# Convolution as diagonal matmuls on TensorE, FP4 tiles cut into three pieces, and rows of B and C loaded per scan unit, in the state-space stage of a hybrid four-part kernel

## The reference, cut to what matters

```python
# L0_attn
xz = einsum('bld,ed->ble', x, W_in);  x_in, z = xz[..., :512], xz[..., 512:]
xc = conv_general_dilated(x_in^T, conv_w, (1,), [(3, 0)], feature_group_count=512) + conv_b   # 4 taps
u  = silu(xc)
x_dbl = einsum('bld,ed->ble', u, W_xproj)           # 16 columns of step size, 16 of B, 16 of C
delta = softplus(einsum('blr,dr->bld', delta_raw, W_dt) + b_dt)
def step(h, inp):                                   # scan over 512 tokens, state 512 x 16
    h = exp(d_t * A) * h + (d_t * u_t) * B_t
    y_t = sum_n h[:, n] * C_t[n]
y = (ys + D_param * u) * silu(z)
out = einsum('bld,ed->ble', y, W_out)
# L0_ffn
scale = max(max(abs(block of 16)) / 6, 1e-12);  q = nearest FP4 value of block / scale, times scale
h = silu(q(x) @ q(w_gate)) * (q(x) @ q(w_up));  out = q(h) @ q(w_down)     # 704 hidden columns
```

## Time and profile before

| | us |
|---|---|
| median of 3 runs | 3855.11 (3853.64 to 3855.38) |
| the profiled execution | 3852.84 |
| its span | 3850.7 |
| busy: PE, DVE, ACT, POOL | 3230.5, 2634.9, 1656.0, 1587.6 |
| first scan of the stage starts at | 124.44 |
| last gate_y of the stage starts at | 1574.76 |

### The profile page before, as it was taken

One profiled execution on the slowest core, in us unless ns is written; L12 is line 12 of the kernel. 1 busy time (PEld: TensorE's weight loads), 2 busy tenths in 40 slices (PEclk: granted clock), 3 DMA queues, 4 the chain that ended last, 5 costly groups with the idle time before them and its releaser, 6 DMA issues. The chain is left out here.

```text
span 3850.7 us, 48624 instructions
## 1 busy us (share of the span) xinstructions
PE 3230.5 (84%) x15980; PEld 1864.1 (48%) x15980; DVE 2634.9 (68%) x3666; ACT 1656.0 (43%) x4077; POOL 1587.6 (41%) x974
## 2 busy tenths in 40 slices
PE   2677787778787778599999959999999689999998
PEld 1224242424242434366666626666666355655665
DVE  6798989888888989477677725555555255555553
ACT  1554545454545454166555613333333133333332
POOL 1555554655455545200000035554455165555552
PEclk9889898988888888899999969999999899999999
DMA  1211111020202020100010020000000200000000
GB/s 47 99 44 61 47 58 72 32 93 11 93 11 93 11 88 11 41 29 26 22 33 27 12 75 12 21 16 16 16 16 11 68 17 22 22 22 22 22 16 17
DMA packets 82137, 141.89 MB, mean 37 GB/s; under 512 B 7730, under 2 KB 71302, under 8 KB 73878
## 3 DMA queue, kind: packets, MB, share of 16 engines
q1 hardware_dynamic: 73622, 132.66, 9.7%
q10 hardware_dynamic: 8448, 8.39, 0.7%
HBM read 119.54 MB, written 21.50 MB: 37 GB/s over the span
## 5 line engine op out<-in xcount | busy, mean ns | idle before, releaser
L902 PE MATMUL ps_y<-hb,ident 128*128 128x512 f32 x1024 | 588.0, 707 | 228.0 <-DVE hb L602 227.8
L492 POOL TENSOR_TENSOR hb<-bcB,du 128x1024 f32<-128x1024 f32 x256 | 604.3, 2374 | 374.0 <-PE ps_y L902 370.6
L592 DVE TENSOR_TENSOR_SCAN ps_dA<-ps_dA,hb 128x1024 f32<-128x1024 f32 x256 | 585.9, 2289 | 90.5 <-POOL hb L492 56.5
L902 PEld LDWEIGHTS ps_y<-hb,ident 128*128 128x128 f32 x1024 | 211.0, 221 | 510.3 <-DVE hb L602 305.3
L1691 POOL TENSOR_TENSOR c_pr<-c_pr,c_inv 128x512 f32<-128x512 f32 (+1 forms) x256 | 232.6, 934 | 411.6 <-DVE c_inv L1803 409.6
L2158 PE MATMUL c_ps_s<-c_hT,c_w 128*128 128x512 f32 x704 | 321.0, 603 | 17.2 <-DVE c_hid L1869 15.4
L1261 ACT ACTIVATE b_pr<-b_ps_s,b_negmax 128x256 f32<-128x256 f32 (+1 forms) x512 | 263.8, 527 | 164.8 <-DVE b_negmax L1175 162.9
L725 ACT ACTIVATE ps_dA<-delta,a_neg 128x511 f32<-128x511 f32 x512 | 329.4, 675 | 0.6
L1920 ACT ACTIVATE c_pr<-c_ps_s,c_negmax 128x256 f32<-128x256 f32 (+1 forms) x512 | 222.2, 446 | 246.5 <-DVE c_negmax L1798 246.5
L602 DVE TENSOR_TENSOR hb<-ps_dA,bcC 128x1024 f32<-128x1024 f32 x256 | 312.3, 1220 | 5.2
L1668 POOL TENSOR_TENSOR c_q_cos<-c_q_cos,c_q_sin 128x1024 f32<-128x1024 f32 x64 | 150.9, 2357 | 311.9 <-DVE c_q_sin L1777 311.9
(11 more groups left out here) (235 smaller groups left out, 6265.2 us busy)
## 6 DMA issues: line engine op xcount, KB each, us to landing
bcB<-bc_scratch SPq DMA_DIRECT2D x32, 1024.0 KB, 4.6
bcC<-bc_scratch SPq DMA_DIRECT2D x32, 1024.0 KB, 6.5
c_x<-stream_scratch SPq DMA_DIRECT2D x16, 512.0 KB, 5.0
c_xr<-stream_scratch SPq DMA_DIRECT2D x16, 512.0 KB, 4.4
xn<-in_x_dram SPq DMA_DIRECT2D x8, 512.0 KB, 7.2
xr<-in_x_dram SPq DMA_DIRECT2D x8, 512.0 KB, 4.0
x_scratch<-xr SPq DMA_DIRECT2D x8, 512.0 KB, 2.9
b_x<-x_scratch SPq DMA_DIRECT2D x8, 512.0 KB, 4.1
```

The costliest lines, as they stand in the source:

```text
L492: pool.tensor_tensor(hb[:, s % RING, :, :], bcB[:, states(g), :], bc(du[:, c % 2, :].unsqueeze(1), [P, NG, T]), ALU.mult)\
L592: dve.tensor_tensor_scan(flat(h_all), flat(h_all), flat(tile), 0.0, ALU.mult, ALU.add)\
L902: last = pe.matmul(ps_y[:, :], W["ident"][:, :], hb[:, r % RING, i, :], start=False, stop=(g == GROUPS - 1 and i == NG - 1))
```

## The change

It rewrites the schedule of the state-space stage and leaves the other stages as they are.

- **Convolution.** The four taps per chunk are no longer DVE operations. Sixteen diagonal matrices diag_c are built once, and per chunk PE runs four matmuls of 128 x 512 into ps_p; ACT applies silu straight from PSUM. Chunks 2 and 3 go through a side buffer u23 and are copied into u later (MOVE_U).
- **FP4 tiles.** fp4_steps becomes fp4_part: the maximum, scale and reciprocal in one unit, the division, exponent and step in the next, and the rounding in the third. This holds for the four h tiles and for x. h has two buffers.
- **B and C.** The buffers bcB and bcC hold four units of two rows each instead of all 16. Each unit loads its own two rows of B and two of C, 512 KB each, so 64 DMAs per batch instead of 8. B of unit s + 6 is issued in SP's step s after POOL has multiplied unit s + 2, C of unit s + 4 after DVE has weighed unit s.
- **Ring.** hb has 8 slots instead of 5.
- **Tables.** All pieces are moved. gate_y comes in the first unit of the next chunk instead of the second. Tiles 1 to 3 of the FP4 layer go to units 21 to 31; the last h tile is transposed in unit 4 of the next batch, and x1 moves to units 1, 2, 4 and 6. softplus of chunk 0 of the next batch is finished in this batch. silu(z) is taken straight from PSUM.

```diff
+def fp4_part(dve, st, rows, blk, work, p, n, part):
+    g = n // 16
+    amax, scale, inv = blk[0:p, 0, 0:g], blk[0:p, 1, 0:g], blk[0:p, 2, 0:g]
+    w = work[0:p, 0:n]
+    blocks = rows.rearrange("p (g e) -> p g e", e=16)
+    if part == 0:
+        st.link(dve.tensor_reduce(amax, blocks, AX.X, ALU.max, apply_absolute_value=True))
+        st.link(dve.tensor_scalar(scale, amax, 1.0 / 6.0, 1e-12, ALU.mult, ALU.max))
+        st.link(dve.reciprocal(inv, scale))
+        return st.done(dve.tensor_scalar(inv, inv, 1.0 - 2.0 ** -24, None, ALU.mult))
+    if part == 1:
+        dve.wait_ge(st.s, st.at(st.k))
+        st.link(dve.tensor_tensor(blocks, blocks, bc(inv.unsqueeze(2), [p, g, 16]), ALU.mult))
+        st.link(dve.tensor_scalar(w.bitcast(U32), rows.bitcast(U32), EXPONENT, None, ALU.bitwise_and))
+        return st.done(dve.tensor_scalar(w, w, 1.0, 1.5 * 2.0 ** 22, ALU.max, ALU.mult))
+    dve.wait_ge(st.s, st.at(st.k))
+    st.link(dve.tensor_tensor(rows, rows, w, ALU.add))
+    return dve.tensor_tensor(rows, rows, w, ALU.subtract)
...
-    RING = 5
-    GATE, SILU = [0, 3, 7, 11], [1, 3, 7, 11]
-    UP = [2, 4, 8, 12]
-    HIDDEN = [4 * t + 3 for t in range(TT)]
-    TURN_H, TAKE_H = [5, 9, 13, 17], [6, 10, 14, 18]
-    X1, TAKE_X1 = [3, 4, 7, 8], [5, 9]
-    Z, TAKE_Z = [20, 20, 24, 1], [21, 21, 26, 2]
-    STATS, TURN_XN, TAKE_XN = 6, 11, 12
-    XQ, TURN_XQ, TAKE_XQ = 16, 20, 21
-    XIN, TAKE_XIN = [16, 16, 18, 18], [17, 17, 19, 19]
-    CONV = [18, 19, 20, 21]
-    U, U3 = 22, 29
-    XD, TAKE_XD = 23, 24
-    DT = [25, 25, 27, 15]
-    ABS, LN, ADD = [26, 26, 28, 16], [27, 27, 3, 16], 20
-    SOFT = [("abs", 0), ("relu", 0), ("abs", 1), ("relu", 1), ("exp", 0), ("exp", 1), ("ln", 0), ("ln", 1),
-            ("abs", 2), ("relu", 2), ("exp", 2), ("ln", 2), ("abs", 3), ("relu", 3), ("exp", 3), ("ln", 3)]
+    RING, ROWS = 8, 4
+    GATE, SILU, UP = [0, 18, 22, 26], [1, 19, 23, 27], [2, 20, 24, 28]
+    HIDDEN = [3, 21, 25, 29]
+    TURN_H, TAKE_H = [9, 24, 28, 4], [10, 25, 29, 5]
+    X1, TAKE_X1 = [1, 2, 4, 6], [4, 8]
+    Z, TAKE_Z = [12, 22, 26, 0], [13, 23, 27, 1]
+    STATS, TURN_XN, TAKE_XN = 1, 6, 7
+    XQ, TURN_XQ, TAKE_XQ = 13, 30, 31
+    XIN, TAKE_XIN = [8, 8, 12, 13], [9, 9, 13, 14]
+    CONV, U = [10, 11, 14, 15], [11, 12, 15, 16]
+    MOVE_U = [20, 28]
+    XD, TAKE_XD = 17, 18
+    STORE = 9
+    DT, ABS, LN = [20, 21, 30, 8], [21, 22, 31, 9], [23, 23, 10, 10]
+    ADD = [26, 4, 13, 14]
+    SOFT = [("abs", 0), ("relu", 0), ("exp", 0), ("abs", 1), ("relu", 1), ("exp", 1), ("ln", 0), ("ln", 1),
+            ("abs", 2), ("relu", 2), ("exp", 2), ("abs", 3), ("relu", 3), ("exp", 3), ("ln", 2), ("ln", 3)]
...
-        bcB = sb("bcB", [P, NS, T])
-        bcC = sb("bcC", [P, NS, T])
+        bcB = sb("bcB", [P, ROWS, NG, T])
+        bcC = sb("bcC", [P, ROWS, NG, T])
...
+            def spread_b(n, s):
+                g = s % GROUPS
+                sp.dma_start(bcB[:, s % ROWS, :, :], bc_dram[n, 1 + g * NG:1 + (g + 1) * NG, :].unsqueeze(0).broadcast_to([P, NG, T]))\
...
+                for s in range(-2, SCANS):
+                    r = s + 2 + ROWS
+                    if r < SCANS:
+                        sp.wait_ge(dBu_ready.s, dBu_ready.at(b, s + 3))
+                        spread_b(b, r)
+                    elif r < SCANS + ROWS and more:
+                        sp.wait_ge(dBu_ready.s, dBu_ready.at(b, s + 3))
+                        if r == SCANS:
+                            sp.wait_ge(bc_out.s, bc_out.at(b + 1, 16))
+                        spread_b(b + 1, r - SCANS)
+                    r = s + ROWS
+                    if 0 <= s and r < SCANS:
+                        sp.wait_ge(weighed.s, weighed.at(b, s + 1))
+                        spread_c(b, r)
+                    elif 0 <= s and more:
+                        sp.wait_ge(weighed.s, weighed.at(b, s + 1))
+                        spread_c(b + 1, r - SCANS)
+                    if s == STORE and prev:
+                        tail(b - 1)
+                    if s == STORE + 2:
+                        sp.wait_ge(stored.s, stored.at(b, 0))
+                        sp.dma_start(xr[:, :, :], io["x"][b].rearrange("(t p) d -> p t d", p=P)).then_inc(xr_in.s, 16)
+                    if s == TAKE_XD + 1 and more:
+                        put_bc(b + 1)
...
-                        if c == 0:
-                            pool.wait_ge(bc_in[g // 2].s, bc_in[g // 2].at(b, 32))
+                        pool.wait_ge(b_in[s % ROWS].s, b_in[s % ROWS].at(b, landed(s)))
                         if s >= RING:
                             pool.wait_ge(summed.s, summed.at(b, s - RING + 1))
-                        else:
-                            pool.wait_ge(summed.s, summed.at(b, 0))
-                        pool.tensor_tensor(hb[:, s % RING, :, :], bcB[:, states(g), :],
+                        elif prev:
+                            pool.wait_ge(summed.s, summed.at(b - 1, SCANS + s - RING + 1))
...
-                if s in CONV:
-                    c = CONV.index(s)
-                    dve.wait_ge(xin_ready.s, xin_ready.at(n, c + 1))
-                    if c == IC - 1:
-                        to = u3[:, :]
-                        dve.wait_ge(u3_ready.s, u3_ready.at(n, 0))
-                    else:
-                        to = u[:, c, :]
-                        if not isinstance(n, int) or n:
-                            dve.wait_ge(du_ready.s, du_ready.at(n - 1, c + 1))
-                            dve.wait_ge(y0_done.s, y0_done.at(n - 1, c + 1))
-                    xs.link(dve.tensor_scalar(to, xin[:, c, 0:T], conv_w[:, c, 0:1], None, ALU.mult))
-                    for j in range(1, 4):
-                        ins = dve.scalar_tensor_tensor(to, xin[:, c, j:j + T], conv_w[:, c, j:j + 1], to,
-                                                       ALU.mult, ALU.add)
-                        if j < 3:
-                            xs.link(ins)
-                        else:
-                            ins.then_inc(cv_ready.s, 1)
+                    if s == XQ:
+                        dve.wait_ge(xn_ready.s, xn_ready.at(n, TT))
+                        dve.wait_ge(xn_turned.s, xn_turned.at(n, DC))
+                    last = fp4_part(dve, xs, rows, blk_x, work, P, TT * D, s - XQ)
+                    if s == XQ + 2:
+                        last.then_inc(xg_ready.s, 1)
...
+                    if HIDDEN[t] <= s < HIDDEN[t] + 3:
+                        rows, blk = h[:, t % 2, :], blk_h[:, t % 2, :, :]
+                        if s == HIDDEN[t]:
+                            if t == 0:
+                                hs.turn(b)
+                            dve.wait_ge(sg_ready.s, sg_ready.at(b, t + 1))
+                            dve.wait_ge(gated.s, gated.at(b, 2 * t + 2))
+                            if t:
+                                dve.wait_ge(h_turned.s, h_turned.at(b, 2 * t - 2))
+                            elif prev:
+                                dve.wait_ge(h_turned.s, h_turned.at(b - 1, 2 * TT - 2))
+                            dve.tensor_tensor(rows.rearrange("p (a n) -> p a n", a=2), ps_p[:, :, 0:HALF],
+                                              sg[:, :].rearrange("p (a n) -> p a n", a=2), ALU.mult).then_inc(h_ready.s, 1)
+                            dve.wait_ge(h_ready.s, h_ready.at(b, t + 1))
...
-                    if g == 1 and c:
+                    if g == 0 and c:
                         gate_y(b, c - 1)
-                    if s == 1 and prev:
+                    if s == 0 and prev:
                         gate_y(b - 1, IC - 1)
-                    ffn(b, s)
+                    ffn(b, s, prev)
...
+                    dve.wait_ge(c_in[s % ROWS].s, c_in[s % ROWS].at(b, landed(s)))
+                    dve.tensor_tensor(tile, h_all, bcC[:, s % ROWS, :, :], ALU.mult).then_inc(weighed.s, 1)
...
+                    if s == U[c]:
+                        act.wait_ge(cv_ready.s, cv_ready.at(n, c + 1))
+                        if c >= 2:
+                            to = u23[:, c - 2, :]
+                            act.wait_ge(u_moved.s, u_moved.at(n, 0))
+                        else:
+                            to = u[:, c, :]
+                            if not isinstance(n, int) or n:
+                                act.wait_ge(du_ready.s, du_ready.at(n - 1, c + 1))
+                                act.wait_ge(y0_done.s, y0_done.at(n - 1, c + 1))
+                        act.activation(to, ps_p[:, c % 2, :], ACT.Silu, bias=cols[:, 0, c:c + 1]).then_inc(u_ready.s, 1)
...
+                    if s == CONV[c]:
+                        pe.wait_ge(xin_ready.s, xin_ready.at(n, c + 1))
+                        for j in range(4):
+                            last = pe.matmul(ps_p[:, c % 2, :], diag_c[:, c, j, :], xin[:, c, j:j + T], start=(j == 0), stop=(j == 3))
+                        last.then_inc(cv_ready.s, 1)
...
-                                pe.wait_ge(z_ready.s, z_ready.at(b, IC))
```

(4 more changed lines are left out.)

381 lines of the change are left out of this document (194 added, 187 removed).

## The result

The changed kernel takes 3792.85 us (median of 4 runs, 3790.99 to 3796.17), the kernel before 3855.24 (3853.64 to 3858.64) beside it: a ratio of 0.984, with a 95% interval of 0.983 to 0.985. The profiled execution took 3792.24 us, its span 3790.1. Forecast were 3772 for the median and 3770 for the profiled execution, so 62.4 us were gained and not 83.

The account below looks back on a forecast made before the run. DVE, the busiest engine of the state-space stage, was taken as the bound. Steady batches sum to 174.5 us, so seven batches save 86.6; net -82.8 us gives 3770 profiled, 3772 median, range 3705 to 3842.

Parts of the forecast that it names:

- DVE's work: Steady batch of the state-space stage: 148.3 us of DVE work that the change keeps, with FP4 tiles priced whole.
- wait for POOL's hb, unit 0: Batch start: POOL scales the old batch's last h tile before du and the first hb, so DVE waits 4.0 us.
- wait for up, unit 3: Unit 3: ACT's work, PE's first x1 tile, addition and up take 13.8 us against DVE's 10.8; wait 3.0.
- wait at gate_y, unit 8: Unit 8: the third x1 tile waits for ACT's copy of the last h tile; gate_y waits about 7.5 us.
- waits for ACT (and the gate in unit 24): Steady batch: table loads and activations make DVE wait 1.5 and 1.8 us, then 1.4 in unit 23; together 4.7.
- lengthening: Parts two and three of five FP4 tiles, ten pieces, meet POOL's multiplications in some 6 of 10 cases; 7 us per batch.
- batch 0, last batch: Batch 0 has no x1, 164.6 us; the last has no preparation, 139.2 of work plus waits and lengthening, 152.4.
- lead-in: Before the first scan: 16 diagonal products on DVE (3.5 us) and the convolution on PE ahead of softplus; 2.5 later.
- One of the prediction's own signs of being wrong: gate_y waiting in units 16, 24 or 0 would show the forecast wrong; no size was given.
- The ring: The wider hb ring gives POOL more lead, but no end is set by it; costed at 0.
- The rival on contention: Slower: each of ten pieces waits 1.8 us or more, at the full 2.33 a batch is 191, kernel 3887; chance 0.06.
- The table drain: Slower rival: about 1.38 us on top of every ACT table load, some 14 per batch, kernel 3865; chance 0.03.

## Why the prediction was right or wrong

The profiled execution is 22 us above the sum. By its terms:

| term of the sum | forecast | measured |
|---|---|---|
| DVE's work | 148.3 | 145.4 |
| wait for POOL's hb, unit 0 | 4.0 | 4.3 |
| wait for up, unit 3 | 3.0 | 3.2 to 4.8 |
| wait at gate_y, unit 8 | 7.5 | 8.0 to 9.5 |
| waits for ACT (and the gate in unit 24) | 4.7 | about 4.0 |
| lengthening | 7 | 10.5 |
| steady batch | 174.5 | 176.8 (mean of six) |
| batch 0, last batch | 164.6, 152.4 | 163.1, 157.5 |
| lead-in | +2.5 | +9.1 |
| tail | +1 | -0.5 |

**Right**: the convolution leaves DVE and is hidden on PE (256 matmul records, 114.8 us, 14.4 per batch against 14 forecast). The waits for POOL in unit 0, for up in unit 3 and at the gate of unit 8 stand where they were put, behind the engine that was named, within about 2 us, and those for ACT in units 12 and 13 and the one in unit 24 or 25 come to 4.0 instead of 4.7. The chain for unit 8, the third x1 tile behind ACT's copy in its pieces of unit 5, is confirmed by the run that moved that one wait.

**Some luck.** A steady batch is 2.3 us over the sum because two errors of its terms partly cancel. Waits and lengthening together are 31.3 where 26.2 were summed. DVE's work is 2.9 less: the sum priced whole tiles, 148.3, and this is what the run with whole tiles shows, but cutting them saves 2.9 more. One of the prediction's own signs of being wrong also came: in five of the eight batches gate_y waits in unit 24, for 0.6 to 1.7 us. It changed little, because in the two steady batches without it the scan of unit 25 waits 1.46 instead.

**The lead-in** was mis-sized by 6.6. The step counted work on DVE and PE. It left out that POOL's hb was no longer last: ACT walks through all its pieces of the lead-in, among them a silu of z, a softplus and the copies of the quantised x, before it makes decays at all. The run with the decays ahead moved the first scan by 7.0, to 2.2 behind the kernel before, close to the 2.5 of the sum.

**The last batch** was 5 short: its waits ahead of up and of the gate of unit 8 were 1.5 and 1.1 longer, and the last gate_y of all waits 3.87 for PE, where the sum had nothing and the kernel before 2.08.

**Lengthening** was 3.5 short, and on the wrong instructions. The step said "now in ten pieces (parts two and three of five tiles)", met in 6 of 10 cases by POOL. In the steady batches of the change these pieces are free (L125 has a mean of 908 ns, L129 of 874, and not the 0.3 to 0.7 us more that the prediction gave as a sign), and the small scalings of the first piece pay. The Trainium skill's page "SBUF — State Buffer", section "Who interferes with whom", which the prediction drew on, still fits: by it a DVE instruction with two SBUF inputs or in a two-port mode is blocked fully, and a reduction never. L119, a reduction, is 0.89 throughout, and L120 ends 0.04 us behind POOL; whether L120 runs in a two-port mode no row shows. What was missing is when POOL runs, and that isn't a chance of 6 in 10: it runs in one stretch behind each wait it has, and stands at the next. Nor are wait and lengthening separate terms: in unit 3 both end with POOL's run.

**The ring** was "no end is set by it, 0". This step failed in kind, as far as four slots show it; the five of the kernel before were not run with the other parts. The ring sets only a small end (1.7 us per batch), yet it decides in which pieces POOL runs, and with four slots the kernel is slower than before. The rival on contention had named the ring of eight as what would let POOL meet the pieces; the runs show the reverse for the pieces, and the four-slot ring is the kernel that this rival describes (a steady batch of 187.7, against its 191). **The split** had no term of its own and is worth 98 us. The sum came close because it was made for all parts at once, unit by unit; taken as a price list of parts it would have been far off.

The table drain doesn't show here either, as in the earlier trace rows. A load and the Exps behind it, ACT in batch 6 of the change:

```profile
1247.47 1.28 ACT L782 ACT_TABLE_LOAD   x1
1248.76 1.30 ACT L782 ACTIVATE ps_dA<-delta,a_neg 128x511 f32<-128x511 f32 x2
```

The Exps start where the load ends, and the waits for ACT are 4.0 us per batch. The 1.38 us on top of each load, which the Trainium skill's page "ScalarE: Activation LUTs" gives in its section "What ACT_TABLE_LOAD costs", are not in these rows; here the rows decide.

## What to carry to other kernels

When one engine's side job is taken away, ask for each neighbouring engine when it runs and not only how much: a buffer ring or a cut that costs nothing by itself can decide whether two engines meet. Look for waits that guard more than the next instruction reads; one line that moved such a wait was worth 44 us here. Before a wait is taken away, ask what else ends at the same moment: the wait in unit 3 was worth 3.6 us per batch and all of it went into lengthening. Before a step is moved in one engine's order, list who waits for it and what is queued behind that waiter.

## What was not expected of the hardware

A DVE instruction of 0.19 us beside back-to-back multiplications of POOL takes up to 5.12 us in the change: it isn't let in between two of them. In the row of batch 5 above L120 waited out the rest of one and the whole next one, in batch 6 the rest of one and the next two.

PE at a granted clock of 0.57 needs 5.06 us for what takes 2.95 at 1.00, so with the stand of 4.9 us ahead of them they cost 2.1 more. Behind a stand of 2.11 us in the run with the moved x1 wait, the same matmuls took 2.95; behind one of 2.15 in the change they took 4.59, at 0.62. The length of the last stand alone doesn't say which, and that stays open.
